# Eighty matmuls of ones on TensorE ahead of the first weight of an attention and expert kernel

## What is computed

```python
# x, ctx: (128, 128, 256) f32; 16 heads of 16; 8 experts of hidden size 64
q = layernorm(x) @ wq.T + bq; k = ctx @ wk.T + bk; v = ctx @ wv.T + bv      # split into 16 heads
x = x + softmax(q @ k.T / 4) @ v @ wo.T + bo
top1 = argmax(layernorm(x) @ Wg.T)
y = gelu((layernorm(layernorm(x)) * ln_scale[top1] + ln_bias[top1]) @ W1[top1] + b1[top1]) @ W2[top1] + b2[top1]
out = x + y
```

## Time and profile before

| | before |
|---|---|
| median of three runs | 1431.42 us |
| lowest and highest run | 1429.01 and 1433.12 us |
| the profiled execution's own time | 1428.45 us |
| its span, first to last instruction | 1426.6 us |
| TensorE busy | 1379.0 us, 97% of the span |
| VectorE busy | 1167.6 us, 82% |
| ScalarE busy | 984.6 us, 69% |
| mean granted TensorE clock | 0.996 |

### The profile page before, as it was taken

How to read it: one execution, slowest core, us unless ns; L and a number is a source line. 1 busy time by engine, 2 the same in 40 slices (tenths; PEclk the granted TensorE clock), 3 DMA queues, 4 the chain that set the end, 5 groups by cost and what they waited for, 6 DMA issues and landing times.

```text
span 1426.6 us, 39972 instructions
## 1 busy us (share of the span) xinstructions
PE 1379.0 (97%) x15314; PEld 1195.5 (84%) x15314; DVE 1167.6 (82%) x2760; ACT 984.6 (69%) x1664; POOL 483.5 (34%) x662
## 2 busy tenths in 40 slices
PE   6899999999999999999999999989999999999998
PEld 5788888888888888888888888877888888888887
DVE  4688888888888888888888888887788878888776
ACT  4577777677777777777777777755767666676764
POOL 4223323233232333233223323224444444444430
PEclk9899999999999999999999999999999999999999
DMA  6566665666656665667656665543343434334322
GB/s 179 136 161 177 168 189 137 172 161 176 172 145 167 173 178 147 166 172 177 160 152 170 175 176 139 160 130 104 100 121 103 135 104 120 113 112 131 102 82 75
DMA packets 167845, 207.44 MB, mean 145 GB/s; under 512 B 18871, under 2 KB 118506, under 8 KB 167658
## 3 DMA queue, kind: packets, MB, share of 16 engines
q1 hardware_dynamic: 167658, 204.89, 53.3%
HBM read 69.26 MB, written 33.81 MB: 72 GB/s over the span
## 4 chain that ended last, share of the span: by engine, by line
PE 79%; DVE 14%; issue 3%; ACT 2%; DMA 1%; POOL 0%; SPq 0%; ACTq 0%; DVEq 0%; POOLq 0%
PE s_ps L1336 13%; PE pp_ps L1210 9%; PE pp_ps L1183 7%; PE pv_ps L1158 7%; PE st_ps L1144 6%; PE s_ps L1116 6%; PE st_ps L1361 6%; PE pp_ps L1218 6%; PE pp_ps L1361 6%; DVE negmax L821 6%; PE pv_ps L1166 4%; DVE cT_lo L847 3%; PE pp_ps L1300 2%; DVE negmax_wide L824 2%; PE pp_ps L1204 2%
## 5 line engine op out<-in xcount | busy, mean ns | idle before, releaser
L637 ACT ACTIVATE pT<-st_ps 128x1024 f32<-128x1024 f32 x256 | 262.9, 1027 | 104.8 <-PE st_ps L1144 103.4
L821 DVE TENSOR_REDUCE negmax<-s_ps 128x8 f32<-128x1024 f32 x256 | 311.4, 1216 | 23.6 <-PE s_ps L1116 23.6
L506 POOL TENSOR_TENSOR xb<-xin,bo_all 128x256 f32<-128x256 f32 x128 | 90.8, 731 | 263.2 <-DMA x_scratch<-xb 178.4
L494 POOL TENSOR_TENSOR q_parts<-q,q_parts 128x1024 bf16<-128x1024 f32 x32 | 68.5, 2139 | 298.3 <-ACT q_parts L631 298.3
L693 ACT ACTIVATE pT<-s_ps,c 128x512 f32<-128x512 f32 x128 | 87.9, 689 | 118.0 <-PE s_ps L1336 112.8
L1116 PE MATMUL s_ps<-k_packed,q_packed 96*128 96x128 bf16 x2048 | 158.5, 220 | 10.5 <-DVE negmax L821 6.1
L1336 PE MATMUL s_ps<-k_packed,w_hi 128*128 128x512 f32 x512 | 164.7, 413 | 0.0
L1144 PE MATMUL st_ps<-q_packed,k_packed 98*128 98x128 bf16 x2048 | 158.1, 220 | 0.0
L1116 PEld LDWEIGHTS s_ps<-k_packed,q_packed 96*128 96x128 bf16 x2048 | 128.4, 98 | 29.0 <-DVE negmax L821 18.4
L1144 PEld LDWEIGHTS st_ps<-q_packed,k_packed 98*128 98x128 bf16 x2048 | 120.7, 98 | 25.4 <-issue 25.4
L1158 PE MATMUL pv_ps<-pT,v 128*32 128x128 f32 x4096 | 138.4, 276 | 0.0
(11 more groups left out here) (199 smaller groups left out, 3690.6 us busy)
## 6 DMA issues: line engine op xcount, KB each, us to landing
q_packed<-q_parts SPq DMA_DIRECT2D x192, 256.0 KB, 3.8
k_packed<-k_parts SPq DMA_DIRECT2D x192, 256.0 KB, 4.4
xin<-in_x_dram SPq DMA_DIRECT2D x32, 512.0 KB, 3.9
cin<-in_ctx_dram SPq DMA_DIRECT2D x32, 512.0 KB, 4.0
x_scratch<-xb SPq DMA_DIRECT2D x32, 512.0 KB, 4.6
out_dram<-xb SPq DMA_DIRECT2D x32, 512.0 KB, 3.2
k_parts<-mask_scratch SPq DMA_DIRECT2D x32, 256.0 KB, 4.0
q_parts<-mask_scratch SPq DMA_DIRECT2D x30, 256.0 KB, 4.1
```

The costliest lines, as they stand in the source:

```text
L506: last = g.tensor_tensor(xb[n % 2][:, b, :], xin[n % 2][:, b, :], bo_all[:], ALU.add)
L637: a.activation(pT[u % 2][:], st_ps[:], ACT.Exp, scale=DH ** -0.5).then_inc(s_exp, 1)
L821: v.tensor_reduce(own, s_ps[:].rearrange("p (h s) -> p h s", s=P), AX_X, ALU.max, negate=True).then_inc(s_red, 1)
```

## The change

VectorE writes ones_bf in place of POOL, as the first instruction of its list, ahead of b2f. TensorE waits for it and then multiplies ones_bf by itself 80 times, each a bf16 matmul of 128 by 128 with 128 columns moving, into the first 128 columns of pv_ps. Nothing reads these products. Only then does it wait for ident and the first weight.

```diff
+        WARM = 80
@@ pool
-            g.memset(ones_bf[:], 1.0).then_inc(s_ones, 1)
@@ vector
+            v.memset(ones_bf[:], 1.0).then_inc(s_ones, 1)
             v.memset(b2f[:], 0.0).then_inc(s_b2z, 1)
@@ tensor
+            pe.wait_ge(s_ones, 1)
+            for k in range(WARM):
+                t.matmul(pv_ps[:, 0:P], ones_bf[:], ones_bf[:], start=True, stop=True)
             pe.wait_ge(s_pc, 5)
             for k in range(4):
                 turn_weight(k)
```

## The result

| | before | after |
|---|---|---|
| median (18 runs each) | 1431.37 us | 1427.25 us |
| lowest and highest | 1428.63, 1433.24 | 1425.50, 1430.84 |
| profiled span | 1426.6 us | 1423.6 us |
| ratio to before, 95% interval | | 0.9972 [0.9965, 0.9979] |

The changed kernel is 4.1 us, or 0.28%, faster. That is inside the 0.3% that I called indistinguishable and outside my range of 1427.6 to 1434.4, by 0.35 us on the fast side. In four later comparisons the ratio was 0.9981, 0.9965, 0.9967 and 0.9971, each interval clear of 1. So the effect is small but real, and the forecast of none was wrong. The execution of the changed kernel that was profiled here, 1425.50 us, is the fastest of its 18.

The account below looks back on a forecast made before the run. TensorE bounds the kernel, busy 1379.0 of 1426.6 us, so the change only moves the loop's start. The front summed to -0.2 us (-0.45 to +0.5), taken as zero: 1431.4 us, range 1427.6 to 1434.4.

Parts of the forecast that it names:

- The memset: Start of the kernel: ones_bf ready on VectorE at about 1.05, TensorE begins at about 1.1; nothing for other engines.
- The 80 matmuls: Warm-up before the first weight: ends at 7.5 us, or 7.2 to 8.2 by the clock's rise, 9.7 with none.
- the late case: Warm-up: clock rises only after 5.5 us of matmuls, ones end at 8.2, ScalarE's first copy 0.5 us late.
- The transposes: First weight's four transposes take 0.64 us at the higher clock in place of 1.10, a gain of 0.46.
- What comes behind: After the first weight: TensorE continues at 12.3 to 13.0; clock low again before q, whose matmuls keep their pace.
- The sum for the front: Prologue up to q: -0.2 us, with -0.45 and +0.5 as ends; taken as zero.
- Rival A: Prologue: clock stays up until q is made, 2.4 to 2.6 us faster, up to 3.5; 1428.6 us; chance 0.15.
- Rival B: Front: warm-up runs past the first weight's arrival, +0.5 to +2.4 us; about 1433 us; chance 0.20.
- upper end: Front: the clock does not rise at all, ones end at 9.7 us, costing +2.4 us.
- Instructions: Front: TensorE's 160 more instructions run while it waited; a late fetch would cost tenths; nothing taken.
- rival C: After 39 us: low-clock stretches fall elsewhere, 1.5 to 3 us either way; chance 0.15 with a visible shift.
- Carrying one to one: Whole kernel: what the prologue gains or loses by the first scores reaches the end in full.

Follow-up runs that it names:

- with fills: Changed kernel plus 28, 16 and 14 more matmuls of ones in TensorE's waits at 10.5, 13.4 and 16 us; 0.9973 of the kernel before.
- WARM = 160: Changed kernel with 160 warm-up matmuls of ones in place of 80; 1.0017 of the kernel before.
- every gap filled: Changed kernel with 28, 16 and 14 matmuls of ones in early waits and 42, 15, 30 and 18 in later ones; 1425.30 us, 0.9948 of the kernel before.
- the wide fills: Changed kernel with the same gaps filled, mostly by 512-column matmuls of ones, so fewer instructions; 1425.57 us, 0.9957 of the kernel before.

## Why the prediction was wrong, point by point

**The memset.** Right: 0.17 us on VectorE, TensorE begins at 1.05 (1.1 forecast), the other engines don't notice.

**The 80 matmuls.** Right in pace, and nearly in place. They end at 7.2, 7.2, 8.1, 8.3 and 8.5 us in the five profiles (7.2 to 8.2 forecast, 9.7 had the clock not risen): the clock rose 3.1 to 6.0 us after they began, where 3.5 to 5.5 had been taken, so two of the five ran up to 0.3 us past the late case. The first weight is used at 7.5 us on average in the kernel before, so the profile that I worked from was favourable there by 0.2 us.

**The transposes.** Right: 0.64 us for four. The Trainium skill's sentence that the full clock does not engage for transposes (TensorE: Matmul & The Clock Gate, Part 4) is not borne out: eight take 1.09 us behind the warm-up and 1.97 us without it. (ScalarE's copy ended at 9.1 us in the first profile, not "at 9.3 at the earliest": a slip in the sum, since 7.95 and 1.11 are 9.06. Nothing hangs on it.)

**What comes behind.** Right: the clock is down again when q is made, in all five profiles of the changed kernel (it fell between 12.9 and 14.5 us). The sum for the front was zero, and the measured mean shift at k's last matmul is -0.1 us. That it comes so near is in part luck, for the single profiles of either kernel lie up to 1.7 us apart there. Rival A did not happen; with fills it could be brought about, and there too q came 2 us earlier. Rival B happened in its small form, a first weight 0.4 us later on average. Its upper end did not happen; its price is what WARM = 160 paid.

**Instructions.** Here the prediction failed. It said of the 160 more instructions that "a fetch that came late there would cost tenths, no row shows it, and I take nothing". It looked for the fetch's cost only where the instructions were added. With it went the sentence that an earlier q and k "moves that whole stretch" of copies: that stretch was taken as fixed in length, and it was not. The last copy of k landed 13.9 us behind the first one's issue before and 12.2 after, in mean. What they did was to move each later fetch, and the first of them, at 29.3 us, lay on a stretch of the prologue that is full on all sixteen DMA engines (from 29 to 31 us the copies' packets took 102% of the sixteen engines' time) and that the scores wait for. The profile's page had the row, 125 packets on the instruction queue, and the trace their times. The term was -1.5 us in the prologue, not zero. About -1.9 us more lie in the loop; that they are of the same kind goes with the count of instructions, but is argued. The first scores, forecast at 40.2 to 41.2 us, came at 38.7, 38.9, 40.1, 40.2 and 41.0. The Trainium skill (Runtime: NRT & Kernel Launch, Instruction fetch mechanics) says that an engine streams its instructions in blocks of 16 KB and that crossing a boundary is mostly hidden. The size agrees with the packets here. That the cost is hidden holds for TensorE, which was busy in 2.00 of the 2.00 us from 29 to 31 in the kernel before, but not for the copies beside it.

**Size.** The accounting of the profiles is -0.1 (warm-up) - 1.5 (fetch in the prologue) - 1.9 (loop) = -3.5 us; the medians say -3.1 to -5.7 in five comparisons. What is beyond 3.5 stays open. The time from the first scores to the end moved by less than the 3 us that rival C allowed, but by another cause than C's, as far as the table goes.

**Carrying one to one** held for the late front (4.4 us, of 6.6 in all; the last copy of k landed another 2.4 us later behind the first, 14.6 against 12.2). The later stretches at the lower clock, which rival C priced at 2.7 and 1.7 us, are gone with every gap filled, and the kernel is 7 us under the one before. The price itself is shown only in part: the first eight steps of the maxima took 24.6 us there and 26.0 with the wide fills, where the kernel before took 26.9 to 27.3.

## What to carry to other kernels

Before costing an edit that only adds instructions to an engine, find that engine's instruction fetches in the DMA view and ask which full stretch of copies they sit in before and after: a shift by a fraction of a block can outweigh what the edit does. A control with as many instructions and no work, and one with the work in fewer instructions, tell the two apart. And a warm-up pays only if the clock is held until the work that needs it: 80 matmuls alone gave 0.1 us by k, and fills in every wait brought 7 us.

## What the runs showed of the hardware

- One 16 KB instruction packet took 0.9 to 1.4 us on its DMA engine. With one among the twelve copies of 256 KB, or just ahead of k's first, the last copy of k landed 13.4 to 14.6 us behind the issue of the first (eleven profiles); without, 12.0 to 12.3 (seven).
- The moments at which the clock steps are not set by the kernel. The same program's first rise was at 22.3, 24.0, 22.6 and 10.8 us. In the last of these TensorE had run nothing but transposes before the rise.
- Eighty matmuls with 32 columns of weights and one moving column took 2.29 us and left the clock where it was, until 22.6 us.
